# A cross-attention block on one core: a padded transpose of the score maxima, and the attention-weighing matmuls moved to other places in TensorE's queue

## The reference, cut to what matters

```
x1 = layer_norm(x, ln1_w, ln1_b)
q, k, v = heads(x1 @ q_w + q_b), heads(ctx @ k_w + k_b), heads(ctx @ v_w + v_b)
scores = q @ k.T / sqrt(16), masked
out = softmax(scores) @ v
hidden = out @ cproj_w + cproj_b + x
y = gelu(layer_norm(hidden, ln2_w, ln2_b) @ fc_w + fc_b) @ proj_w + proj_b
return hidden + y
```

## Time and profile before

| | |
|---|---|
| runs shown, median (lowest to highest) | 236.17 us (235.68 to 238.47), 3 runs |
| the profiled execution, its own time | 235.78 us |
| its span | 234.0 us |
| busy: TensorE matmul, VectorE, ScalarE, GpSimd | 214.8, 173.0, 125.5, 92.4 us |

### The profile page before, as it was taken

One profiled execution on the slowest core, in us unless ns is written; L12 is line 12 of the kernel. 1 busy time (PEld: TensorE's weight loads), 2 busy tenths in 40 slices (PEclk: granted clock), 3 DMA queues, 4 the chain that ended last, 5 costly groups with the idle time before them and its releaser, 6 DMA issues.

```text
span 234.0 us, 8336 instructions
## 1 busy us (share of the span) xinstructions
PE 214.8 (92%) x3520; PEld 199.0 (85%) x3520; DVE 173.0 (74%) x376; ACT 125.5 (54%) x269; POOL 92.4 (39%) x101
## 2 busy tenths in 40 slices
PE   6768995697999999999999999999999999998995
PEld 6757974686999899998999899889998998897995
DVE  2587567586989768985988598967896569777571
ACT  3458466046824795279606962588248833561240
POOL 5445416429941285109520761247313621313300
PEclk9999999799999999999999999999999999999999
DMA  6957995920000581039301860068003900100101
GB/s 192 261 197 181 242 270 156 243 52 4 3 3 1 164 211 41 3 101 232 83 1 49 233 134 3 3 199 213 3 1 95 212 20 1 53 0 3 39 6 48
DMA packets 21979, 23.13 MB, mean 99 GB/s; under 512 B 1558, under 2 KB 20662, under 8 KB 21942
## 3 DMA queue, kind: packets, MB, share of 16 engines
q1 hardware_dynamic: 21008, 21.84, 36.3%
q10 hardware_dynamic: 934, 0.75, 1.1%
HBM read 7.62 MB, written 2.10 MB: 42 GB/s over the span
## 4 chain that ended last, share of the span: by engine, by line
PE 64%; DMA 9%; DVE 8%; ACT 8%; issue 7%; POOL 1%; ACTq 1%; SPq 1%; POOLq 0%
PE bank L1065 19%; PE bank L1067 15%; PE bank L1066 15%; PE bank L1142 7%; DMA stack_kq<-n_t 4%; DMA ctx_in<-in_ctx_t 4%; PE scores L1095 3%; ACT probs L614 2%; ACT parts L588 2%; PE bank L1082 2%; DVE z_lo L937 2%; PE bank L1209 1%; ACT z_hi L633 1%; POOL rs L557 1%; PE scores L1124 1%
## 5 line engine op out<-in xcount | busy, mean ns | idle before, releaser
L1065 PE MATMUL bank<-z_hi,fc_hi 128*128 128x256 f32 x128 | 37.8, 295 | 2.0 <-DVE z_lo L937 1.9
L1065 PE MATMUL bank<-proj_hi,g_hi 128*128 128x256 f32 x128 | 38.0, 297 | 1.7 <-DVE g_lo L891 1.6
L872 DVE RECIPROCAL recip<-bank 128x256 f32<-128x256 f32 x16 | 28.0, 1753 | 13.2 <-PE bank L1142 13.2
L1067 PE MATMUL bank<-proj_lo,g_hi 128*128 128x256 f32 x128 | 35.7, 279 | 0.0
L1067 PE MATMUL bank<-z_lo,fc_hi 128*128 128x256 f32 x128 | 35.7, 279 | 0.0
L1066 PE MATMUL bank<-proj_hi,g_lo 128*128 128x256 f32 x128 | 35.7, 279 | 0.0
L1066 PE MATMUL bank<-z_hi,fc_lo 128*128 128x256 f32 x128 | 35.7, 279 | 0.0
L557 POOL TENSOR_TENSOR rs<-ve,power 128x1 f32<-128x1 f32 x16 | 9.8, 614 | 52.6 <-DVE ve L852 52.6
L628 ACT ACTIVATE fc_raw<-bank,fc_bias 128x256 f32<-128x256 f32 x64 | 26.6, 469 | 5.6 <-PE bank L1067 5.5
L571 POOL TENSOR_TENSOR o_lo<-o,o_hi 128x256 fp32r<-128x256 f32 x16 | 16.5, 1029 | 30.7 <-ACT o_hi L621 30.6
L1065 PEld LDWEIGHTS bank<-z_hi,fc_hi 128*128 128x128 f32 x128 | 24.0, 187 | 3.9 <-DVE z_lo L937 2.5
(11 more groups left out here) (125 smaller groups left out, 578.1 us busy)
## 6 DMA issues: line engine op xcount, KB each, us to landing
stack_kq<-parts SPq DMA_DIRECT2D x48, 256.0 KB
x_in<-in_x SPq DMA_DIRECT2D x8, 256.0 KB, 3.2
ctx_in<-in_ctx_t SPq DMA_DIRECT2D x7, 256.0 KB, 3.7
out<-y SPq DMA_DIRECT2D x7, 256.0 KB, 2.2
fc_raw<-in_fc_w SPq DMA_DIRECT2D x1, 1024.0 KB, 9.9
proj_raw<-in_proj_w SPq DMA_DIRECT2D x1, 1024.0 KB, 10.0
ctx_in<-in_ctx_t ACTq DMA_DIRECT2D x1, 256.0 KB, 4.2
w_raw_q<-in_q_w SPq DMA_DIRECT2D x1, 256.0 KB, 4.8
```

Source lines behind the costliest of these rows:

```text
L872: ve.reciprocal(recip[:], bank7[:, 1, :, :]).then_inc(recip_made, 1)
L1065: mm(out_ap, a_hi, b_hi, start=first, stop=False, skip_group_check=True)
L1067: return mm(out_ap, a_hi, b_lo, start=False, stop=last, skip_group_check=True)
```

## The change

Two things are changed.

The weights of `turn_maxima` become 128 columns wide. The tile `n_parts` is now a view of the first 32 columns of a zeroed tile `n_wide` of 144 columns, and each of the two matmuls takes 128 columns from its place on. The result has 128 partitions, of which the first 16 are read as before. VectorE zeroes the two tiles at the start of the program, before its first other work.

In `full_step`, TensorE's order changes. `weigh(b, 0)` stands directly behind `shift(b, 1)`, ahead of the wait for z2 and `fc_chunk(c, 0)`, where it stood behind that chunk. `weigh(b, 1)` stands behind `fc_chunk(c, 3)`, where it stood ahead of it, and `first_score(a)` follows it at once, where it stood between `mlp_chunks` 0 and 1. The last steps keep their order.

```diff
-        n_parts = [sb(f"n_parts{p}", [P, KC, N_PARTS, H // KC], BF16) for p in range(TT)]
+        n_wide = [sb(f"n_wide{p}", [P, N_PARTS * H + P - N_PARTS * H // KC], BF16) for p in range(TT)]
+        n_parts = [n_wide[p][:, 0:N_PARTS * H].rearrange("p (m k h) -> p m k h", m=KC, k=N_PARTS) for p in range(TT)]
...
+        n_turn_ps = bank4[:, 0, 0:KC * P]
...
             def first_step(a):
+                for n in n_wide:
+                    ve.memset(n[:], 0.0).then_inc(n_wide_zeroed, 1)
+                dve.wait_ge(n_wide_zeroed, TT)
...
                 for m in range(KC):
-                    last = mm(n_t_ps[:, P * m:P * m + P], n_parts[p][:, m, :, :].rearrange("p k h -> p (k h)"), ident_b[:],
+                    first = N_PARTS * H // KC * m
+                    last = mm(n_turn_ps[:, P * m:P * m + P], n_wide[p][:, first:first + P], ident_b[:],
...
                 shift(b, 1)
+                weigh(b, 0)
 
                 pe.wait_ge(z2_split, c.count(1, 1))
...
                 fc_chunk(c, 0)
-                weigh(b, 0)
...
                 fc_chunk(c, 2)
-                weigh(b, 1)
                 pe.wait_ge(gelued, c.count(4, 2))
                 fc_chunk(c, 3)
+                weigh(b, 1)
+                first_score(a)
                 project(b, 0, a)
...
                 mlp_chunks(c, (0,))
-                first_score(a)
                 mlp_chunks(c, (1,))
```

More of the change, by code:

```diff
@@ L227, in build @@
         mask_ready = sem("mask_ready")
+        n_wide_zeroed = sem("n_wide_zeroed")
         vb_repeated = sem("vb_repeated")
```

## The result

The changed kernel takes 240.14 us (median of 4 runs, 239.46 to 240.72) against 235.93 (4 runs, 234.05 to 238.47): a ratio of 1.0213, 95% interval 1.0169 to 1.0258. It is slower, by an amount whose interval lies on both sides of 2%. Every ratio in this document leaves out executions that fell in a slower state (more than 1.5% above the fastest of the same kernel, as 238.47 here), so it is not the quotient of the two medians. Forecast was 240.4. The profiled execution took 240.06 us, its span is 238.3.

What follows compares the result with a forecast made beforehand. TensorE, busy 92%, was taken to bound the kernel, with ScalarE's and VectorE's fixed orders adding waits. Terms 0.9 + 4 x 0.58 + 0.4 + 1.1 - 0.1 = +4.6 us on 235.8 gave 240.4 us, range 236.6 to 242.6.

Steps and rivals of the forecast that it cites:

- First weighing behind the shift: TensorE, steady step: weighing 0 starts 0.62 after the shift, fc chunk 0 1.03 later without its z_lo wait; gain 0.58 us.
- Wait for gelu 1: Before fc chunk 3, which overwrites the bank gelu 1 reads: a new TensorE wait of 0.84 us plus 0.10 restart.
- Wait for g_lo: Before MLP chunk 1: a second new wait of 0.62 us, as VectorE's split is queued behind its second reciprocal.
- Turns: Padded turns of the maxima on TensorE: 0.43 instead of 0.64 us for tile 1, saving 0.21; tile 0 saves 0.09.
- Small DMA: Maxima's DMA before the second shift: wait of 0.52 in step 2, 0.15 in four others; sum 1.1 us.
- Steady step: One full step: 0.88 us longer from the second shift on, less 0.21 and 0.09 for the turns: +0.58 us.
- First and last: First full step +0.9 us, last +0.4, three shorter turns in the second step -0.1; the start's memsets nothing.
- 1: Rival: only TensorE's removed changes of matmul kind count, 1.08 us saved a step, 230.4 us; chance 0.03.
- 2: Rival: the gelu wait comes but the g_lo wait does not, each step 0.62 shorter than forecast, 236.7 us; chance 0.10.
- 3: Rival: the first score, some 2 us sooner, waits for its stacked operands, 0.5 us per affected step, 243 us; chance 0.05.

Runs made afterwards that it cites:

- e8: Changed kernel with the second weighing and first score put back to their old places, first weighing still behind the shift: 232.31 us, ratio 0.9868 to the kernel before.
- e2: Changed kernel with ScalarE's gelu chunk 1 moved directly behind chunk 0, ahead of the copies of v and rounding of o: 232.99 us, ratio 0.9935.
- e3: Changed kernel with VectorE's split of gelu chunk 1 moved ahead of the second reciprocal: 235.19 us, ratio 1.0003 to the kernel before.
- e1: Kernel before plus the padded turn alone, TensorE's order as before: 236.52 us, ratio 1.0056.
- e6: e1 with the wide tiles allocated last, so all other tiles keep their old addresses: 235.32 us, ratio 1.0011 to the kernel before.
- e7: Changed kernel with the wide tiles allocated last, so all other tiles keep their old addresses: 238.84 us, ratio 1.0163 to the kernel before.
- e10: e8 with the wide tiles allocated last, so all other tiles keep their old addresses: 231.55 us, ratio 0.9838 to the kernel before.
- e5: Old order and old narrow turn, but wide tiles allocated as in the change, moving later tiles by 448 bytes: 236.19 us, ratio 1.0039 to before.
- e4: Changed kernel with both reorderings, ScalarE's from e2 and VectorE's from e3: 231.88 us, ratio 0.9865 to the kernel before.

## Why the prediction was right

It gave 240.4 us and the terms behind it; 240.14 was measured. By its steps:

- *First weighing behind the shift:* 0.63 and 1.03 measured for 0.62 and 1.03, no bracket ahead of chunk 0, gain 0.58 by the forecast. e8 shows the half by itself. Right.
- *Wait for gelu 1:* forecast 0.84 plus 0.10; measured 0.92 by the bracket and what it hides. From the start of gelu 0 to the end of gelu 1 it was 3.51 (110.31 to 113.82) for the forecast 3.39. The sum was 0.12 short, and 0.09 of that is a slip: the 0.72 from the start of gelu 0 to the start of the copies already leaves out their overlap of 0.09, and I took it off the copies' 1.49 once more. Put right it is 3.48; the last 0.03 is a gap between two of ScalarE's instructions. e2 takes the wait away by ScalarE's order alone. The mechanism is right, the size a little too small.
- *Wait for g_lo:* forecast 0.62; measured 0.60 in five steps and 0.50 in the third, where the score came 1.13 behind the weighing (115.49 to 116.62) instead of 1.03, so that TensorE was ready later (see the rivals below for why). The two distances that make the wait are exact: 1.17 from the weighing to the reciprocal (115.49 to 116.66) and 3.27 from there to the end of g_lo, for 3.26. e3 takes it away by VectorE's order alone. Right.
- *Turns:* 0.42 and 0.34 measured (tile 1, and tile 0 from 122.09 to 122.43) for 0.43 and 0.33. The sizes are right. (The 0.056 of a keep-clock matmul was had with one distance too few in the divisor, since 20 matmuls have 19; the distance from the first of them to the full matmul behind them, 49.60 to 50.71, gives 0.056 as well.) That they shorten the step holds only where the weighing stands ahead of z_lo's wait, as in the changed kernel; e1 and e6 show that alone they are worth nothing. I had not said so, and it made me miss e1.
- *Small DMA:* forecast 0.52 in step 2 and 0.15 in four others, 1.1 in all; measured 0.38 more in steps 2 and 5 and nothing in the rest, 0.76 in all. The mechanism is right, the size was 0.3 too large. Which steps have the wait was not foreseen: in e7 it is the third alone (0.48), in e10 the second, and why it moves is open.
- *Steady step:* forecast +0.58; measured +0.66 in step 3. From the second shift to MLP chunk 1 it is 13.08 us (106.91 to 119.99) where it was 12.00: +1.08 for the forecast 0.88. Nearly all of the 0.20 is there when the second weighing starts (8.58 behind the shift for the forecast 8.39), 0.12 of it the sum over ScalarE's row. The rest of the step gives back 0.42, where the turns were to give 0.30: the kernel before had a wait there that I had not seen. It is for the split of MLP chunk 3, and so short that no bracket shows it. First before, then after:

```profile
122.34 0.60 PE L1082 MATMUL bank<-ident,z 128*128 128x128 f32 x4
122.83 0.38 PE L1065 MATMUL bank<-proj_hi,g_hi 128*128 128x256 f32 x1
```

```profile
124.59 0.60 PE L1088 MATMUL bank<-ident,z 128*128 128x128 f32 x4
124.94 0.37 PE L1071 MATMUL bank<-proj_hi,g_hi 128*128 128x256 f32 x1
```

The four transposes take 0.49 before and 0.35 after: 0.14 was a wait under the bar. In step 4 of before the same place has a bracket, which is why that step took 25.08 and grew by 0.24 only:

```profile
147.84 0.39 PE L1065 MATMUL bank<-proj_hi,g_hi 128*128 128x256 f32 x1 [0.23 <-DVE g_lo L891]
```

- *Spacing:* a term that the forecast lacks. A step has 144 full matmuls; at 0.1183 for 0.1170 us that would be 0.19 a step, but part of it falls into waits: the traces show some 0.11 a step without the reordering (e5 against before, e1 against e6) and 0.06 with it (e7), where a step takes 25.26, +0.60 over the kernel before.
- *First and last:* forecast +0.9 in the first step, measured +0.68; forecast +0.4 from the last on, measured 0.65 + 0.34 = 0.99; forecast -0.1 up to the first turn, measured -0.29. The 0.34 behind the last turn is the addresses: with the old ones that stretch takes 35.18 before, 35.17 in e6, 35.14 in e7 and 35.16 in e10, with the tiles moved 35.44 in e5, 35.47 in e1, 35.52 in the changed kernel and in e8. The last step's 0.65 for 0.4 was not taken apart.
- *Rivals:* 1 fell on the two waits. 2 fell on the reciprocal's 1.17. 3 is real and was kept small by the gelu wait. Its margin of 1.8 us, read from the DMA share falling near 113.3, was not there: in the changed kernel's third step the first score starts only when the stack DMA releases it, 9.71 us behind the shift, where the forecast had it at 9.42. That is the 1.13, a wait of 0.10 that only the row of the weight loads shows:

```profile
116.62 0.58 PEld L1101 LDWEIGHTS scores<-stack_kq 97*64 97x64 bf16 x32 [0.19 <-DMA stack_kq<-parts]
```

  e7 has it in its second step (0.29 by the bracket), and with the gelu wait gone it costs 0.5 to 1.0 in four steps of e2. In the changed kernel's other steps no such wait shows. That its 243 us did not come is thus owed to the gelu wait, which holds TensorE back, and not to the margin that I gave it: right by luck.

So the total, +4.3 of the span for the forecast +4.6, is right by two waits sized to within 0.1 and, luck on top, by smaller errors that cancel. Steps 2 to 5 were forecast at 4 x 0.58 + 1.1 = 3.4 and took 2.9 more: the DMA 0.3 too large and the old waits for g_lo left out, against the gelu wait sized too small and the spacing left out. The end was 0.6 too small.

## What to carry to other kernels

When matmuls are moved in the queue of the engine that bounds, ask of each block what it covered where it stood: here a second weighing of 1.03 us was the time in which a gelu emptied the bank for the next chunk, and 0.20 us of saved changes of kind cost two waits of 0.9 and 0.6 us. Then ask what the engines fed by it have queued, in their own fixed order, behind the instruction that it releases; either their orders are changed with it (e4), or only the half is moved that uncovers nothing (e10, 1.6% faster). Test a change of several moves in halves, since a gain and a loss of 4 and 8 us had been added up here, and allocate a new tile behind the others so that it doesn't move them.

## What the runs showed of the hardware that I had not expected

- The addresses of tiles in on-chip memory change the pace of full matmuls. With what lies behind the maxima's tiles moved by 448 bytes, 128x128 weights on 256 columns follow each other at 0.1183 to 0.1184 us instead of 0.1170 to 0.1172, and the mean duration in the profile goes from 279 to 281 ns (e5 against e7). It costs 0.4% of the time with nothing else changed (e5: 1.0039, 1.0011 to 1.0067).
- Most of what the turn cost hung on the width of its weights, and not on their type (bf16 between other types): with 128 columns it starts 0.12 us behind the last full matmul, like a full one, and its two matmuls take 0.10 (127.75, 127.87, 127.97), where with 16 columns these were 0.21 and 0.21 (125.60, 125.81, 126.02). Behind it the first full matmul is still followed only after 0.20 us (127.97 to 128.17) instead of 0.118, as it was before (0.22). Together 0.42 for 0.64.
- Issuing a DMA from ScalarE's queue takes 0.63 us of that engine (127.79 in e1), which the busy time leaves out and the next instruction's bracket books on another engine.
